# The last three layers of a twelve-layer model in one loop over the steps of a sort

## Chip, cores and metric

The kernel runs on one core of a Trainium2 chip. The metric is the device time of one execution in microseconds (us). An engine is named as the profile names it: PE is TensorE, DVE is VectorE, ACT is ScalarE, POOL is GpSimd, SP issues transfers.

## The reference

Twelve residual layers run over x, 32 tiles of 128 tokens by 128 features. Each layer is `x = x + f(layernorm(x))`. The change touches only the last three:

```python
def sparsemax(z):                       # attention over 32 patterns, 16 heads
    z_sorted = -jnp.sort(-z, axis=-1)
    cum = jnp.cumsum(z_sorted, axis=-1)
    support = 1.0 + k * z_sorted > cum
    k_sup = jnp.sum(support, axis=-1, keepdims=True)
    tau = (jnp.take_along_axis(cum, k_sup - 1, axis=-1) - 1.0) / k_sup
    return jnp.maximum(z - tau, 0.0)
# layer 9:  A = sparsemax(scale * (h @ Wq + bq) . keys); out = (A @ values) @ Wo + bo
# layer 10: probs = softmax(h . ctx / 32) * dropout_mask; out = (probs @ ctx) @ Wout.T + bout
# layer 11: x_scale = max(amax(|h|), 1e-6) / 127; x_q = clip(round(h / x_scale), -128, 127)
#           out = (x_q @ weight_q.T) * x_scale * weight_scale + bias
```

## The kernel before

x stays in the on-chip memory for all twelve layers. A layer walks over eight groups of four tiles, so a `128x512` operand is one group. Each layer is a function of its own, written as one instruction list per engine; semaphores order the engines, and every engine takes its own list strictly in the order of the code. A layer ends with a barrier of all engines. Layers 9, 10 and 11 are `sparse_attention`, `attention1(cross=True)` and `quantized`.

**Layer 9.** `sparse_attention` finds the threshold tau by sorting 64 rows of 32 scores per token. The sort is 15 merge steps on DVE (`STEPS`, lines 3375 and 3376: one `max` and one `min` instruction each, over half of the elements). In ten of the steps (`KEEPS`) ACT copies the ends that the step does not compare (line 3295, `keep_ends`), and the step behind it waits for that copy. Then come a running sum (L3385), a multiplication by 1/k (L3386) and a maximum (L3389), which gives tau; DVE subtracts tau from the scores (L3402) and ACT clips them at zero (L3255). PE turns the clipped scores (L3216), multiplies by the values (L3221) and by the output weights in 64 small matmuls (L3227), and turns the result back (L3233). ACT empties each of these from PSUM (L3260, L3265, L3271). While DVE sorts group i, the other engines finish group i-1 and prepare the scores of group i+1 (L3201, L3204, L3207; copies L3278, L3282, L3287). Where ACT does which copy between its `keep_ends` is written out by hand.

**Layers 10 and 11.** Each handles its eight groups in a loop that is one group deep: layernorm on DVE with the power -1/2 on POOL (L130), then a chain that goes back and forth between the engines. In layer 10 it is turn h (L2327), scores (L2351), maximum and subtraction on DVE (L2480, L2481), `exp` on ACT (L2429), sum and dropout mask on DVE (L2486, L2489), turn (L2361), values (L2372), division on DVE (L2496), turn (L2381), output (L2386), two additions on DVE. In layer 11: layernorm, magnitude on ACT (L3497), maximum and scale (L3528 to L3531), round (L3536 to L3539), turn and product (L3472, L3480), two scalings on DVE (L3546, L3551), and two additions on POOL (L3579, L3583). The last store follows the last addition.

Of the kernel before, what the change touches and what calls it, by code (L numbers as in the profile page):

```python
# [14 lines left out]
ALU = mybir.AluOpType  # L15
# [3084 lines left out]
def sparse_attention(nc, name, x, const, w, at):  # L3100

    S = 32
    ROWS = GROUP * HEADS
    LI = 16  # L3110
    scale = float(HD) ** -0.5
    with ExitStack() as ctx:
        L = Layer(nc, ctx, name, at.side)
        stats = L.sbuf("stats", [T, GROUP, 6])
        moments = L.sbuf("moments", [T, GROUP, 2])
        pad = L.sbuf("pad", [T, 1])
        rstd = L.sbuf("rstd", [T, GROUP])
        h = L.sbuf("h", [T, GROUP, D])
        h_t = L.sbuf("h_t", [D, GROUP * T])
# [7 lines left out]

# [3 lines left out]
        tau = L.sbuf("tau", [T, ROWS])  # L3131
# [3 lines left out]
        p_misc = L.psum("p_misc", [T, BANK])  # L3135
        p_q = L.psum("p_q", [T, BANK])
        p_out = L.psum("p_out", [T, GROUP, D])
        p_s = [L.psum(f"p_s{n}", [T, BANK]) for n in range(4)]
        stats_ready = L.sem("stats_ready")
        rstd_ready = L.sem("rstd_ready")  # L3140
        normed = L.sem("normed")
        trans = L.sem("trans")
        h_t_ready = L.sem("h_t_ready")
# [4 lines left out]
        shifted = L.sem("shifted")  # L3148
        clipped = L.sem("clipped")
# [7 lines left out]
        dve_order = L.sem("dve_order")  # L3157
# [5 lines left out]
        started = lambda i: not (isinstance(i, int) and i == 0)  # L3163
# [3 lines left out]
        def step_buffers(q, n):  # L3167

            return (srt[(n - 1) % 2][:, :, :] if n else z[:, q, :, :]), srt[n % 2][:, :, :]
# [12 lines left out]

        with nc.Block() as block:
            @block.sync
            def _(sp):
                at.fetch(sp)

            @block.tensor
            def _(pe):
                pe.wait_ge(at.loaded, at.count)  # L3190
                nc.tensor.matmul(p_misc[:, 0:S], w["wk"][:, :], w["key_t"][:, :], start=True, stop=True)\
                    .then_inc(kv_done, 1)
                pe.wait_ge(kv_ready, 2)
                nc.tensor.matmul(p_misc[:, 0:D], k_rep[:, :, :], w["wv"][:, :], start=True, stop=True).then_inc(kv_done, 1)
                pe.wait_ge(kv_ready, 3)

                def before(j):

                    pe.wait_ge(normed, j + 1)
                    for u in range(GROUP):  # L3200
                        last = nc.tensor.transpose(p_misc[:, u * T:(u + 1) * T], h[:, u, :], const["ident"][:, :])  # L3201
# [34 lines left out]
                def body(i, p, last_group):  # L3236
                    if started(i):
                        pe.wait_ge(z_ready, GROUP * (i + 1))
                        behind(i - 1, 1 - p)
# [696 lines left out]
```

## Time and profile before

| | us |
|---|---|
| median of 3 runs | 3240.82 (3239.86 to 3245.16) |
| the profiled execution, its own time | 3239.51 |
| its span | 3237.7 |
| layers 9, 10 and 11 in the span | 2643.2 to the end, 594.5 |

The span is the stretch from the first to the last instruction of the profiled execution, and all positions below count from its start. The clock of a stretch is a share of PE's full 2.4 GHz. Two views matter. One gives the busy time of each engine in a stretch (the four stretches below are layer 9's start, its sorts and end, layer 10, and layer 11); an engine that is busy nearly all of it bounds that stretch, while three that are each half busy point to a chain that passes from one to the next. The other lists instructions in order of time, so that a start minus the start before it gives what an instruction really takes of its engine, overlap and gap included.

### The profile page before, as it was taken

How to read it: one execution, taken by the hardware profiler on the slowest of the kernel's cores; microseconds unless marked ns; L12 is line 12 of the kernel's file. 1: busy time of each engine (PE TensorE's matmuls, PEld its weight loads, DVE VectorE, ACT ScalarE, POOL GpSimd, SP SyncE). 2: the span in 40 equal slices, each digit the busy share in tenths (PEclk: the TensorE clock that was granted, in tenths of full speed). 3: DMA queues.
4: the chain of work that ended last, by engine and by line, in shares of the span. 5: the costliest groups of instructions: out<-in, count | busy, mean ns of one | idle time of the engine just before them, and what ended most of it. 6: DMA issues, size and time to landing. Idle time of an engine off the chain costs nothing. (4 is left out here: it accounts for less than half of the span.)

```text
span 3237.7 us, 53191 instructions
## 1 busy us (share of the span) xinstructions
PE 2502.4 (77%) x20516; PEld 1453.8 (45%) x20516; DVE 2098.6 (65%) x4141; ACT 1392.3 (43%) x2771; POOL 604.3 (19%) x581
## 2 busy tenths in 40 slices
PE   6777779999699799979979996799779943443461
PEld 3544546666344344435534444456545521332351
DVE  7989945555687455557654434688732249999657
ACT  5565547777222122223334432498613313433311
POOL 2342511111000133324410000111140120000003
PEclk8888879999799899979979998799879976767665
DMA  1000010000000000010000000200101100000110
GB/s 59 2 2 1 2 39 4 8 8 1 4 1 1 31 2 2 2 45 12 9 4 1 0 1 18 89 9 11 47 32 33 39 17 0 1 1 0 37 44 26
DMA packets 41988, 51.90 MB, mean 16 GB/s; under 512 B 9291, under 2 KB 30868, under 8 KB 40724
## 3 DMA queue, kind: packets, MB, share of 16 engines
q1 hardware_dynamic: 39700, 44.39, 4.3%
q0 software_dynamic: 2048, 4.20, 0.4%
q8 instruction: 164, 2.69, 0.4%
q14 instruction: 76, 0.62, 0.1%
HBM read 39.39 MB, written 9.18 MB: 15 GB/s over the span
## 5 line engine op out<-in xcount | busy, mean ns | idle before, releaser
L130 POOL TENSOR_TENSOR l_rstd<-l_moments,const_minus_half 128x4 f32<-128x4 f32 x104 | 115.6, 1111 | 1535.1 <-DVE l_moments L124 1530.0
L1426 PE MATMUL l_p_gate<-l_h_t,w_wg 128*128 128x512 f32 x400 | 209.0, 605 | 0.0
L1449 PE MATMUL l_p_out<-l_hidden,w_wd 128*128 128x512 f32 x400 | 204.4, 594 | 2.5 <-DVE l_hidden L1719 2.4
L804 DVE TENSOR_REDUCE l_top<-l_ring 128x8 f32<-128x1024 f32 x128 | 150.9, 1221 | 79.6 <-PE l_ring L638 79.5
L2956 DVE SCALAR_TENSOR_TENSOR l_mix<-l_decay,l_cb 128x1024 f32<-128x1024 f32 x128 | 173.4, 1370 | 27.1 <-ACT l_decay L2840 22.9
L2840 ACT ACTIVATE l_decay<-l_p_ring 128x1024 f32<-128x1024 f32 x128 | 129.8, 1026 | 129.3 <-PE l_p_ring L2734 128.3
L350 ACT ACTIVATE l_probs<-l_probs,l_minus_top 128x128 f32<-128x128 f32 x512 | 156.8, 393 | 33.6 <-DVE l_minus_top L410 33.6
L1719 DVE TENSOR_TENSOR l_hidden<-l_act_out,l_p_spread 128x512 f32<-128x512 f32 x128 | 85.8, 686 | 128.9 <-ACT l_act_out L1547 128.7
L3216 PE MATMUL l_p_s<-const_ident,l_z 128*128 128x128 f32 x128 | 27.9, 409 | 177.5 <-ACT l_z L3255 177.5
L1209 DVE TENSOR_REDUCE l_minus_top<-l_p_score 128x4 f32<-128x1024 f32 x64 | 78.3, 1224 | 105.8 <-PE l_p_score L1037 102.2
L136 DVE TENSOR_SCALAR l_h<-x_res,l_moments,l_rstd 128x128 f32<-128x128 f32 (+1 forms) x384 | 112.6, 357 | 45.5 <-POOL l_rstd L130 45.2
L1547 ACT ACTIVATE l_act_out<-l_p_gate,w_eb 128x512 f32<-128x512 f32 x128 | 85.6, 686 | 98.3 <-PE l_p_gate L1426 98.2
L753 ACT ACTIVATE l_probs_t<-l_ring 128x1024 f32<-128x1024 f32 x64 | 62.0, 1022 | 149.2 <-PE l_ring L662 149.2
L3375 DVE TENSOR_TENSOR l_srt<-l_srt 128x1024 f32<-128x1024 f32 (+3 forms) x112 | 115.8, 1034 | 14.8 <-ACT l_srt L3295 11.0
L753 ACT ACTIVATE l_probs_t<-l_ring,l_mask_col 128x1024 f32<-128x1024 f32 x64 | 67.8, 1111 | 121.9 <-PE l_ring L662 121.9
L1140 ACT ACTIVATE l_probs<-l_p_score,l_minus_top 128x256 f32<-128x256 f32 x256 | 118.3, 484 | 1.7 <-DVE l_minus_top L1209 1.7
L888 POOL TENSOR_TENSOR l_spread_q<-l_q_t,const_slot_of 128x512 f32<-128x512 f32 x64 | 66.7, 1042 | 278.0 <-PE l_ring L662 278.0
L3376 DVE TENSOR_TENSOR l_srt<-l_srt 128x1024 f32<-128x1024 f32 (+3 forms) x112 | 114.9, 1026 | 0.0
L1449 PEld LDWEIGHTS l_p_out<-l_hidden,w_wd 128*128 128x128 f32 x400 | 75.3, 190 | 84.4 <-issue 52.3
L3216 PEld LDWEIGHTS l_p_s<-const_ident,l_z 128*128 128x128 f32 x128 | 25.7, 223 | 183.3 <-issue 154.8
L1426 PEld LDWEIGHTS l_p_gate<-l_h_t,w_wg 128*128 128x128 f32 x400 | 72.2, 193 | 78.1 <-issue 64.3
L405 DVE TENSOR_TENSOR l_probs<-l_p_score,l_bias 128x1024 f32<-128x1024 f32 x64 | 78.0, 1219 | 37.3 <-PE l_p_score L258 37.3
(471 smaller groups left out, 6260.9 us busy)
## 6 DMA issues: line engine op xcount, KB each, us to landing
l_c_t<-in_ctx_t SPq DMA_DIRECT2D x24, 256.0 KB, 2.8
l_rows_in<-l_zero SPq DMA_DIRECT2D x1, 2432.0 KB
l_tile_h<-l_rows_in SPq DMA_DIRECT2D x38, 64.0 KB, 1.9
l_rows_out<-l_tile_y SPq DMA_DIRECT2D x38, 64.0 KB, 1.5
w_mask<-in_mask SPq DMA_DIRECT2D x1, 2048.0 KB, 9.2
w_wg<-in_l2f_wg SPq DMA_DIRECT2D x1, 2048.0 KB
w_wu<-in_l2f_wu SPq DMA_DIRECT2D x1, 2048.0 KB
w_wd<-in_l2f_wd SPq DMA_DIRECT2D x1, 2048.0 KB
```

Of the source, the lines that this page charges most:

```text
L130: return nc.gpsimd.tensor_tensor(rstd[:, :], moments[:, :, 1], minus_half[:, 0:moments.shape[1]], ALU.pow)
L136: last = nc.vector.tensor_scalar(h[:, u, :], x[:, i * count + u, :], moments[:, u, 0:1], rstd[:, u:u + 1], ALU.subtract, ALU.mult)
L350: last = nc.scalar.activation(probs[:, g % 4, k, :], probs[:, g % 4, k, :], ACT.Exp, bias=minus_top[:, g % 4, k:k + 1])
L753: nc.scalar.activation(probs_t[:, b % 2, half * HALF:(half + 1) * HALF, :], turned_buffer(b, half)[:, :, :, :].rearrange("p a r q -> p (a ...
L804: nc.vector.tensor_reduce(top[:, b % 2, half * HALF:(half + 1) * HALF, 0], s, AX.X, ALU.max)\
L1140: last = nc.scalar.activation(probs[:, g % 2, k, :], p_score[g % 2][:, odd, b * KEYS:(b + 1) * KEYS], ACT.Exp, bias=minus_top[:, g % 2, k: ...
L1426: nc.tensor.matmul(p_gate[k % 2][:, :], w["wg"][:, s, :], h_t[:, g % 4, :], start=True, stop=True)\
L1449: nc.tensor.matmul(p_out[:, :], w["wd"][:, s, :], hidden[:, k % 4, :], start=(s == 0), stop=(gated and s == steps - 1)).then_inc(down, 1)
L2840: nc.scalar.activation(decay[:, g % RING, :, :], p_ring[slot % 2][:, :, :], ACT.Exp).then_inc(evicted, 1)
L2956: nc.vector.scalar_tensor_tensor(mix[:, g % RING, :, :], decay[:, g % RING, :, :], 1.0, bcast(cb[:, i % 2, n // 4, :], [T, QH, T], 1), ALU ...
L3375: nc.vector.tensor_tensor(da, a, b, ALU.max)
L3376: last = nc.vector.tensor_tensor(db, a, b, ALU.min)
```

## The change

The three functions become one, `sparse_cross_quantized`. Every engine's list is now written by a loop over a step number `g`; a sort has 18 steps (15 merge steps, running sum, multiplication, maximum), and `group_at(g, s)` says which group is at place `s` of a timetable that starts with its sort. Layer 10 of a group begins 27 steps behind the start of its sort, and layer 11 at 39. So, while group k+1 is sorted, group k finishes layer 9 and starts layer 10, and group k-1 goes through layer 11.

Four pieces of work also move. The threshold is no longer subtracted by DVE and clipped by ACT before the turning: its negative is turned to rows (`turn_tau`), and PE adds it while turning the scores, by a second matmul with `spread`, which repeats each row of 64 thresholds 32 times; ACT clips while it empties PSUM. The layernorm of layers 9 and 10 is applied by ACT with a per-row scale and bias, for which DVE makes a small `offset`. The sum of the softmax comes out of ACT's `exp` (`accum_out`), and ACT also does the division and the scaling of layer 11 by row. POOL's two additions of layer 11 go to DVE.

```diff
-def sparse_attention(nc, name, x, const, w, at):
+def sparse_cross_quantized(nc, name, x, const, w, at, aps):
...
+        SORTED = len(STEPS)
+        SCAN, INVERSE, TAU = SORTED, SORTED + 1, SORTED + 2
+        PERIOD = TAU + 1
+        BEFORE, BEHIND, IN_CROSS, IN_QUANT = -15, TAU + 1, TAU + 10, TAU + 22
+        def group_at(g, step):
+            k, off = divmod(g - step, PERIOD)
+            return k if off == 0 and 0 <= k < NG else None
...
+                def turn_tau(k):
+                    pe.wait_ge(tau_ready, k + 1)
+                    nc.tensor.transpose(p_out[0:ROWS, 0, :], minus_tau[:, k % 2, :], const["ident"][:, :]).then_inc(tau_turned, 1)
+                def transposes(k):
+                    pe.wait_ge(tau_t_ready, k + 1)
+                    pe.wait_ge(z_ready, GROUP * min(k + 2, NG))
                     for b in range(4):
                         for u in range(GROUP):
-                            last = nc.tensor.transpose(p_s[b][:, u * T:(u + 1) * T], z[:, q, row:row + 4, :],
-                                                       const["ident"][:, :])
+                            nc.tensor.matmul(out, z[:, k % 2, row:row + 4, :], const["ident"][:, :], start=True, stop=False)
+                            last = nc.tensor.matmul(out, spread[:, row:row + 4, :], tau_t[:, :], start=False, stop=True)
                         last.then_inc(turned, 1)
...
+                for g in range(FIRST, END):          # PE; step k of the timetable runs before step k+1
+                    BEHIND: turn_tau;  BEHIND + 1: transposes;  BEHIND + 2, + 3: weigh
...
```

The loop of each engine is a list of such places, shortened here to the places (in brackets: the step of the sort in which the place falls). `BEHIND` is 18 (step 0), `BEFORE` -15 (step 3), `IN_CROSS` 27 (step 9), `IN_QUANT` 39 (step 3).

```
PE:   turn_tau (0) transposes (1) weigh (2, 3) project (5) turn_out (7) turn_h (6) queries (7) scores (8)
      cross_turn_h (12) cross_scores (13) cross_transposes (16) cross_values (17) turn_att (0) cross_output (1)
      turn_quant (8) product (9)
ACT:  keep_ends (each of KEEPS, first in its step) copy_tau (1) clip_turned (2, 3) copy_weighed (4, 5)
      copy_projected (6, 7) norm_apply SPARSE (6) copy_h (7) copy_queries (8) copy_scores (9, 10)
      norm_apply CROSS (12) cross_copy_h (13) exponent (15) cross_copy_turned (17) divide (0) copy_att (1)
      magnitude (6) copy_quant (9) scale_output (10)
DVE:  sort (its step) scan (15) inverse (16) threshold (17) add_output (8) norm_stats SPARSE (3)
      norm_offset SPARSE (5) norm_stats CROSS (9) norm_offset CROSS (11) cross_top (14) cross_mask (16)
      cross_add (2) norm_stats QUANT (3) quant_apply (5) largest (7) round_h (8) quant_add (11)
```

```diff
-                def clip(j, q):
-                    nc.scalar.activation(z[:, q, :, :], z[:, q, :, :], ACT.Relu).then_inc(clipped, 1)
+                def norm_apply(layer, k):
+                    for u in range(GROUP):
+                        last = nc.scalar.activation(h[layer][:, u, :], x[:, k * GROUP + u, :], ACT.Identity,
+                                                    bias=offset[layer][:, u:u + 1], scale=rstd[layer][:, u:u + 1])
+                def clip_turned(k, b):
+                    act.wait_ge(turned, 4 * k + b + 1)
+                    nc.scalar.activation(a_t[:, b, :], p_s[b][:, :], ACT.Relu).then_inc(turned_out, 1)
+                def exponent(k):
+                    for u in range(GROUP):
+                        last = nc.scalar.activation(probs[:, u, :], p_cross[:, u * T:(u + 1) * T], ACT.Exp, bias=minus_top[:, u:u + 1],
+                                                    scale=cross_scale, accum_out=total[:, u:u + 1])
+                def divide(k):
+                        last = nc.scalar.activation(att[:, u, :], p_cross[:, u * D:(u + 1) * D], ACT.Copy, scale=total[:, u:u + 1])
+                def scale_output(k):
+                        last = nc.scalar.activation(out8[:, u, :], p_quant[:, u * D:(u + 1) * D], ACT.Copy, scale=scale8[:, u:u + 1])
...
-                    nc.vector.tensor_tensor(z[:, p, :, :], z[:, p, :, :], bcast(tau[:, :], [T, ROWS, S], 2), ALU.subtract)\
-                        .then_inc(shifted, 1)
+                def cross_add(k):
+                    dve.wait_ge(cross_out, k + 1)
+                    nc.vector.tensor_tensor(update[:, :, :], by_token(p_cross[:, :]), bcast(w["cross_bo"][:, :], [T, GROUP, D], 1),
+                                            ALU.add).then_inc(cross_added, 1)
+                    dve.wait_ge(cross_added, k + 1)
+                    order.then(nc.vector.tensor_tensor(rows_of(k), rows_of(k), update[:, :, :], ALU.add))
+                def largest(k):
+                    dve.wait_ge(mag_ready, k + 1)
+                def quant_add(k):
+                    dve.wait_ge(quant_scaled, k + 1)
...
-LAYERS = {0: layer0, 9: layer9, 1: layer1, 6: layer6, 10: layer10, 11: layer11, ...}
+LAYERS = {0: layer0, 9: layer9, 1: layer1, 6: layer6, ...}
-ORDER = tuple(range(12))
+ORDER = tuple(range(10))
```

How the instructions stand now. First PE between the thresholds of one group and its output matmuls, before; `l_p_s` are the four PSUM banks of the group, `l_z` its scores, `l_o_of` the weighed values:

```order
L3207 MATMUL l_p_s<-l_keys,l_q_t 128x512 x4
L3216 MATMUL l_p_s<-const_ident,l_z 128x128 x16
L3221 MATMUL l_p_s<-l_a_t,l_vals_of 128x512 x4
L3227 MATMUL l_p_s<-l_o_of,w_wo 128x128 x64
L3233 MATMUL l_p_out<-const_ident,l_y_t 128x128 x4
```

And PE at the same place now (the pair of L3304 and L3305 stands 16 times; `l_p_cross` is the one PSUM bank of layer 10):

```order
L3347 MATMUL l_p_cross<-const_ident,l_probs 128x128 x4
L3354 MATMUL l_p_cross<-l_ctx_v,l_probs_t 128x128 x4
L3296 MATMUL l_p_out<-const_ident,l_minus_tau 64x128
L3361 MATMUL l_p_cross<-const_ident,l_att 128x128 x4
L3304 MATMUL l_p_s<-const_ident,l_z 128x128
L3305 MATMUL l_p_s<-l_tau_t,l_spread 128x128
...
L3367 MATMUL l_p_cross<-w_cross_wo,l_att_t 128x128 x4
L3310 MATMUL l_p_s<-l_a_t,l_vals_of 128x512 x4
L3317 MATMUL l_p_s<-l_o_of,w_wo 128x128 x64
```

The output matmuls of layer 10 of the group before (L3367) now stand behind all 16 pairs. On DVE the piece that waits for them is this one, from the maximum that gives tau to the fourth step of the next sort (`l_update` is layer 10's output with its bias):

```order
L3631 TENSOR_REDUCE l_minus_tau<-l_srt 128x64
L3611 TENSOR_TENSOR l_srt<-l_z 128x1024
L3612 TENSOR_TENSOR l_srt<-l_z 128x1024
L3611 TENSOR_TENSOR l_srt<-l_srt 128x512x2
L3612 TENSOR_TENSOR l_srt<-l_srt 128x512x2
L3611 TENSOR_TENSOR l_srt<-l_srt 128x512
L3612 TENSOR_TENSOR l_srt<-l_srt 128x512
L3652 TENSOR_TENSOR l_update<-l_p_cross,w_cross_bo 128x512
L3655 TENSOR_TENSOR x_res<-x_res,l_update 128x512
L3611 TENSOR_TENSOR l_srt<-l_srt 128x256x4
```

Three merge steps stand between the threshold and the addition of layer 10; before, the sort was followed by the subtraction L3402 and nothing of another layer. On ACT the same stretch of a sort, from the copy of the third merge step (L3476 is `keep_ends` now) to that of the eighth:

```order
L3476 COPY l_srt<-l_srt 128x512x2
L3442 ACTIVATE l_a_t<-l_p_s 128x512 x4
L3476 COPY l_srt<-l_srt 128x256x2x2
L3446 COPY l_o_of<-l_p_s 128x32x16 x2
L3476 COPY l_srt<-l_srt 128x256x2
L3446 COPY l_o_of<-l_p_s 128x32x16 x2
L3451 ACTIVATE l_y_t<-l_p_s,w_bo 128x4x4x8 x2
L3432 ACTIVATE l_h<-x_res,l_offset,l_rstd 128x128 x4
L3510 ACTIVATE l_mag<-l_h 128x512
L3476 COPY l_srt<-l_srt 128x128x2x4
```

The copies of the weighed values (L3446) have moved from ahead of the second `keep_ends` to behind the second and third, and the magnitude of layer 11 (L3510), for which DVE waits in step 7, stands behind the first copies of the projection (L3451).

## Rows read from the trace of the kernel before

**Rows 1.** Stretches: us, busy PE, PEld, DVE, ACT, POOL, PE clock, DMA, GB/s.
```profile
2643.00:2662.00 19.00, 10.21 (x19) 4.49 (x19) 9.42 (x41) 3.62 (x6) 2.06 (x2) 0.56 0.03 7
2662.00:3049.98 387.98, 148.18 (x1346) 101.37 (x1346) 349.17 (x364) 158.71 (x226) 6.04 (x6) 0.70 0.00 1
3050.00:3155.40 105.40, 61.89 (x288) 53.92 (x288) 58.02 (x178) 19.78 (x33) 8.06 (x8) 0.64 0.20 62
3155.40:3237.70 82.30, 13.76 (x64) 8.49 (x64) 60.23 (x185) 9.73 (x16) 28.35 (x24) 0.50 0.07 26
```

**Rows 2.** Timeline of one sort period: start us, us, engine, line, operation.
```profile
2708.44 1.22 DVE L3375 TENSOR_TENSOR l_srt<-l_z 128x1024 f32<-128x1024 f32 x1
...
2715.35 1.22 DVE L3375 TENSOR_TENSOR l_srt<-l_srt 128x1024 f32<-128x1024 f32 x1
...
2725.55 0.96 DVE L3375 TENSOR_TENSOR l_srt<-l_srt 128x768 f32<-128x768 f32 x1 [0.55 <-ACT l_srt L3295]
...
2739.55 4.42 DVE L3385 TENSOR_TENSOR_SCAN l_srt<-l_starts,l_srt 128x2048 f32<-128x2048 f32 x1
...
2746.33 2.29 DVE L3389 TENSOR_REDUCE l_tau<-l_srt 128x64 f32<-128x2048 f32 x1
...
2749.26 2.28 DVE L3402 TENSOR_TENSOR l_z<-l_z,l_tau 128x2048 f32<-128x2048 f32 x1
...
2752.78 0.17 DVE L124 TENSOR_SCALAR l_moments<-l_moments 128x4 f32<-128x4 f32 x1
...
2754.07 1.12 DVE L136 TENSOR_SCALAR l_h<-x_res,l_moments,l_rstd 128x128 f32<-128x128 f32 x4 [1.12 <-POOL l_rstd L130]
2755.10 1.22 DVE L3375 TENSOR_TENSOR l_srt<-l_z 128x1024 f32<-128x1024 f32 x1
```

**Rows 3.** Timeline of PE: the small matmuls at either clock.
```profile
2706.97 3.65 PE L3216 MATMUL l_p_s<-const_ident,l_z 128*128 128x128 f32 x16 [19.12 <-ACT l_z L3255]
...
3075.40 1.06 PE L2351 MATMUL l_p_score<-l_k_t,l_h_t 128*128 128x128 f32 x8
...
3138.53 1.91 PE L2351 MATMUL l_p_score<-l_k_t,l_h_t 128*128 128x128 f32 x8
```

**Rows 4.** Timeline of PE: the large matmuls of layer 9 at either clock.
```profile
2681.50 6.35 PE L3207 MATMUL l_p_s<-l_keys,l_q_t 128*128 128x512 f32 x8 [0.78 <-ACT l_q_t L3282]
...
2710.41 3.77 PE L3221 MATMUL l_p_s<-l_a_t,l_vals_of 128*128 128x512 f32 x8
...
2718.16 5.19 PE L3227 MATMUL l_p_s<-l_o_of,w_wo 32*128 32x128 f32 x128 [3.96 <-ACT l_o_of L3265]
...
2728.24 3.70 PE L3207 MATMUL l_p_s<-l_keys,l_q_t 128*128 128x512 f32 x8 [0.78 <-ACT l_q_t L3282]
```

**Rows 5.** Timeline of ACT in one sort period.
```profile
2713.24 1.13 ACT L3295 COPY l_srt<-l_srt 128x1024 f32<-128x1024 f32 x1 [1.99 <-DVE l_srt L3376]
...
2714.25 3.85 ACT L3265 COPY l_o_of<-l_p_s 128x512 f32<-128x512 f32 x4
...
2723.37 1.14 ACT L3271 ACTIVATE l_y_t<-l_p_s,w_bo 128x128 f32<-128x128 f32 x4 [3.08 <-PE l_p_s L3227]
```

**Rows 6.** Groups of instructions by form: count, busy, mean ns of one.
```profile
L2815 ACT ACTIVATE l_conv<-l_p_ring,w_conv_b,w_conv_w 128x512 f32<-128x512 f32 x32 | 25.1, 784 | 0.0
L3282 ACT ACTIVATE l_q_t<-l_p_q,l_scaled_bq 128x512 f32<-128x512 f32 x8 | 5.5, 687 | 7.6 <-PE l_p_q L3204 7.6
```

**Rows 7.** Groups of the last three layers: DVE beside POOL's additions.
```profile
L3536 DVE TENSOR_TENSOR l_q<-l_h,l_amax 128x512 f32<-128x512 f32 x8 | 11.4, 1421 | 0.3
L3551 DVE TENSOR_TENSOR l_out<-l_out,w_scale 128x512 f32<-128x512 f32 x8 | 5.5, 686 | 0.0
```

**Rows 8.** Timeline in layer 0 and at the very end: POOL.
```profile
112.66 1.22 DVE L2956 SCALAR_TENSOR_TENSOR l_mix<-l_decay,l_cb 128x1024 f32<-128x1024 f32 x1
112.82 2.22 POOL L130 TENSOR_TENSOR l_rstd<-l_moments,const_minus_half 128x4 f32<-128x4 f32 x1 [8.71 <-DVE l_moments L124]
...
3233.48 1.26 POOL L3583 TENSOR_TENSOR x_res<-x_res,l_out 128x512 f32<-128x512 f32 x1
```

More of the change, by code:

```diff
@@ L3130, in sparse_attention @@
         starts = L.sbuf("starts", [T, ROWS, S])
-        tau = L.sbuf("tau", [T, ROWS])
+        minus_tau = L.sbuf("minus_tau", [T, 2, ROWS])
+        tau_t = L.sbuf("tau_t", [ROWS, T])
+        spread = L.sbuf("spread", [ROWS, ROWS, S])
+        offset = [L.sbuf(f"offset{n}", [T, GROUP]) for n in range(2)]
         a_t = L.sbuf("a_t", [T, 4, GROUP * T])
@@ L3234, in behind @@
                     last.then_inc(out_done, 1)
[L3236 to L3239, printed above, removed]
-                    if not last_group:
-                        if not started(i):
-                            pe.wait_ge(z_ready, GROUP)
-                        before(i + 1)
-                before(0)
-                for i in range(NG):
-                    body(i, i % 2, i == NG - 1)
@@ new lines, in turn_att, with cross_output @@
+                def turn_att(k):
+                    pe.wait_ge(cross_divided, k + 1)
+                    for u in range(GROUP):
+                        last = nc.tensor.transpose(p_cross[:, u * T:(u + 1) * T], att[:, u, :], const["ident"][:, :])
+                    last.then_inc(att_turned, 1)
+                def cross_output(k):
+                    pe.wait_ge(att_t_ready, k + 1)
+                    for u in range(GROUP):
+                        last = nc.tensor.matmul(p_cross[:, u * D:(u + 1) * D], att_t[:, u * T:(u + 1) * T],
+                                                w["cross_wo"][:, :], start=True, stop=True)
+                    last.then_inc(cross_out, 1)
@@ new lines, in turn_quant, with product @@
+                def turn_quant(k):
+                    pe.wait_ge(rounded, k + 1)
+                    if k >= 1:
+                        pe.wait_ge(quant_scaled, k)
+                    for u in range(GROUP):
+                        last = nc.tensor.transpose(p_quant[:, u * T:(u + 1) * T], q[:, u, :], const["ident"][:, :])
+                    last.then_inc(q_turned, 1)
+                def product(k):
+                    if k == 0:
+                        pe.wait_ge(wq_ready, 1)
+                    pe.wait_ge(q8_t_ready, k + 1)
+                    for u in range(GROUP):
+                        last = nc.tensor.matmul(p_quant[:, u * D:(u + 1) * D], q8_t[:, u * T:(u + 1) * T], wq8[:, :],
+                                                start=True, stop=True)
+                    last.then_inc(quant_out, 1)
@@ L3404, in _, with norm_stats, norm_offset @@
[L3404 to L3407 removed]
+                def norm_stats(layer, k):
+                    layernorm_stats(nc, dve, order, x, k, stats[layer], moments[layer], pad[layer]).then_inc(stats_ready[layer], 1)
+                def norm_offset(layer, k):
+                    dve.wait_ge(rstd_ready[layer], k + 1)
+                    nc.vector.scalar_tensor_tensor(offset[layer][:, :], moments[layer][:, :, 0], -1.0, rstd[layer][:, :],
+                                                   ALU.mult, ALU.mult).then_inc(offset_ready[layer], 1)
```

731 lines of the change are left out of this document (403 added, 328 removed).

## Prediction

> **What bounds the kernel now.** I read the busy times by stretch first, since the shares of the whole page average over twelve layers. In the sorts of layer 9, DVE is busy 349.2 of 388.0 us; PE and ACT are busy 148 and 159 us [rows 1]. That stretch is bound by DVE. In layers 10 and 11 no engine is: DVE is busy 58.0 of 105.4 and 60.2 of 82.3 us, PE 61.9 and 13.8 us [rows 1]. There the chain between the engines sets the pace. So the three layers hold 477 us of DVE work in 594.5 us, and the question is whether the idle 117 us can be closed.
>
> The timeline of one sort period tells what DVE does in it. A period is 46.66 us (2708.44 to 2755.10). The 15 merge steps take 31.1 us, of which 0.55 and some 0.1 are waits for ACT's copies; sum, multiplication and maximum take 9.1 us (2739.55 to 2748.62). Then come an addition of 0.6, the subtraction of the threshold 2.2, the layernorm's statistics 1.5 (2751.46 to 2752.95), 1.1 of waiting for POOL and 1.0 of applying it [rows 2]. The sort alone is thus 30.5 + 9.1 = 39.6 us.
>
> **DVE's work after the change.** Gone from a period are the subtraction, the wait for POOL and the application; an addition (0.7 with its semaphore), the statistics (1.5) and a small offset (0.2) stay: 42.0 us. Layer 10 costs DVE 58.0 / 8 = 7.25 us a group, less a subtraction, a sum and a division of 0.69 each [rows 7] and an application of 1.1 [rows 2]: 4.1. Layer 11 costs 60.2 / 8 = 7.5, less one scaling of 0.69 and the 0.73 by which the rounding multiplication was slowed beside POOL's additions (1.42 against 0.69 [rows 7]), plus the two additions from POOL at 0.69: 7.5. With 0.5 for gaps behind semaphores a full period would hold 54.1 us of DVE. With nothing else in the way the stage would be a start of 21, periods of 42, 45, 5 x 54.1 and 52.4, and an end of 67, in all 498 us. That is 96 us less than now.
>
> **Why I do not expect that.** The engines take their lists in order, and the lists meet at three places. I walk through one full period; t = 0 is the end of the reduction that gives the thresholds.
>
> *PE and the turning.* Before, 16 transposes took 3.65 us at the low clock [rows 3], 0.23 each. Now there are 16 pairs of fp32 matmuls, and an fp32 matmul of this size is two instructions: 8 instructions took 1.91 us at 1.2 GHz and 1.06 us at 2.4 GHz [rows 3], 0.24 and 0.13 each. 64 of them are 15.3 or 8.5 us. PE comes to them from short work with gaps, so at the low clock; in the trace the clock rose 3.4 us after the transposes began (2706.97; the matmuls at 2710.41 run at the high clock [rows 3, 4]), and in the scores at 2681.50 only after nearly 6 us [rows 4]. I take 4.6 us at the low clock and the rest at the high one: 10.5 us. The trace has no fp32 matmul with 64 rows of weights; I price it as one with 128, and nothing in the rows allows less than one instruction's 0.13.
>
> *Stall 1, at `cross_add`.* The mask of layer 10 is ready 2.4 us before t = 0. From there: turn 1.1, copy 0.7, values 2.0, division 1.2 (four instructions in 1.14 [rows 5]), turning of the attention 1.1, so PE reaches the pairs at t = 4.0 and leaves them at 14.5; the output matmuls of layer 10, behind them, end at 15.6. DVE has run three merge steps (2708.44 to 2715.35 [rows 2]) and stands at `cross_add` from t = 6.9. It waits 8.7 us and leaves the two additions at A = 17.2. Behind it wait the sort and every copy of ACT that needs a step.
>
> *Stall 2, at `largest`.* Steps 3 to 7 take 9.6 us (2715.35 to 2725.55 less 0.6 of waits [rows 2]), two sets of statistics 3.0, offset and application 1.2: DVE asks for the magnitude at A + 13.8. ACT's list up to it: `keep_ends` behind step 3, then two copies of weighed values until A + 5.4 (3.85 us for four [rows 5]), `keep_ends` behind step 4 and two more until A + 9.3. PE's 64 matmuls take 5.2 [rows 4] until 14.6; then ACT's copies 0.7, the layernorm 1.6 and the magnitude 0.7: A + 17.6. DVE waits 3.8 us.
>
> *Stall 3, at `quant_add`.* The maximum and its three small instructions take 1.3, step 8 1.9, an addition 0.7, rounding 1.5 (until A + 23.1); then step 9 2.1, statistics 1.5, steps 10 and 11 3.7 and an offset 0.2: DVE reaches `quant_add` at A + 30.7. PE makes queries (2.1) and then the scores from A + 23.5. These took 6.35 us at a mostly low and 3.70 at the high clock [rows 4]; I take 5.6. Turning, copy, product, two score copies and the scaling bring it to A + 32.7: 2.0 us of wait. At the high clock this stall is gone.
>
> What follows until the next threshold is clean: 2.1 for `quant_add`, and 17.0 for steps 12 to 17 with maximum and mask. So the period ends at A + 51.8 = 69.0 us, 15 us above DVE's work.
>
> *What hides.* The four `exp` with a sum (1.1 us by the nearest row [rows 5], twice that if a sum costs another instruction each) run beside the running sum of 4.4 us; without that cover they would cost their length eight times, 9 to 18 us. The layernorm of layer 10 on ACT runs beside step 12, and the three powers have two merge steps each. The transfers of layer 10 move to the start and to one group per period, and a store of a group goes out while the next is sorted; layer 10 used 0.20 of the DMA engines for 105 us [rows 1], so they fit into a period three times. SP's list waits for `added` before it loads the group three further on; that group's data is needed a whole period later. The two barriers between the layers, some 2 us, are in the 594.5 already.
>
> *ACT's new work.* A scale and a bias per row cost ACT about 0.1 us each: 784 ns with both, 687 with one [rows 6]. Four instructions with one take 1.14 us [rows 5], with both I take 1.6. Applying the norm took DVE 1.12 [rows 2]. The Trainium skill, page "ScalarE: Activation LUTs", section "Rules for kernel authors", advises VectorE over ScalarE for additions and multiplications, and the same page puts a pointer operand at 93 ns, with which the trace agrees. By its figures the four would be an estimated 1.6 us too, and the rule speaks against the move only where ACT is late, as it is at stall 2.
>
> **The sum.** The start takes 19 us before [rows 1]; the filling of `spread` (2048 elements; the cheapest and the dearest instruction of that size would be about 1 and 2.3) and the slower application make it 21.3. The first sort waits 2 us for scores at the low clock: 44. The second has no rest of layer 10, but its step 8 waits for the `keep_ends` that stands behind the projection, some 6.6 us: 55. Five full periods: 345. The last one, without a next group: 64. The end: up to `cross_add` of the group before 17; its layer 11 beside the last projection until 35; then the last group's layer 10, 18 from its first copy (turn and copy 2, scores 2, maximum 1, `exp` 1.6, mask 0.7, turn and copy 2, values 2, division 1.2, turn, copy and output 4, additions 1.5), and its layer 11, 13: 66 us, and 3 from the last addition to the end of the span, as now [rows 8]: 69. In all 598.5, against 594.5: 4.0 us more. The profiled execution took 3239.5, 1.3 less than the median of the runs; so 3243.5 beside it, and 3245 as a median.
>
> **The rivals.**
> 1. *The clock is mostly high* (faster). PE has more to do per us than before, when the sorts ran at a mean of 0.70 of full speed [rows 1]. Then the pairs take 8.5, the steps ahead of them 1.4 less, and stall 3 goes: 63.6 us a period, and 3210 in all; halfway between is 3228. Against it: layer 10, with PE busy 62 of 105 us, had 0.64 [rows 1]. I take 3222 for this case. It decides for faster from about 2 us saved in each of six periods.
> 2. *The clock stays low through the pairs.* 15.3 instead of 10.5, seven times and once in the end: 3245 + 34, about 3279.
> 3. *DVE and POOL block each other.* All merge steps read two tensors on chip and now run beside POOL's power. The rows speak both ways: POOL's power took 2.22 us when DVE's two-tensor instruction had started first, and that one its usual 1.22 [rows 8]; but the rounding was slowed by 0.73 beside a POOL addition [rows 7]. If each of some 22 powers costs DVE 0.73, it is 16 us: 3261. The Trainium skill, page "SBUF — State Buffer", section "Who interferes with whom", has the one that issues second wait for the whole of the other; by that rule either could be the loser, and the trace agrees with both sides of it.
> 4. *It does what it says*: no stall, DVE at 54.1 a period, 498 us, 3144. This needs PE through the pairs and layer 10's output by t = 6.9, that is 3 us for 64 instructions.
>
> **How the numbers follow.** Chances: forecast 0.40, rival 1 0.30, rival 2 0.12, rival 3 0.08, rival 4 0.05, and 0.05 for further waits of 15 to 30 us. The forecast's own range is 3234 to 3256. About 0.2% (6.5 us) is what a measurement of this kernel can tell from no change. Faster: nearly all of rival 1, rival 4 and a little of the forecast, 0.35. Within 0.2%: 0.27. Slower: 0.38. The range from 3213 to 3277 leaves out rival 4, the far ends of 1 and 2.
>
> **What the profile would show.** Right: sort periods of 65 to 73 us; DVE waiting 7 to 10 us for the matmuls of `cross_out` once per period from the third sort on, with the 64 instructions of the pairs just before them; 3 to 5 us for ACT's magnitude; up to 3 for ACT's `out8`; no merge step longer beside POOL's power. Wrong: periods near 54 us, or a wait at the copies of the ends that is longer than these three. What would upset the forecast most is the clock in the pairs, since each 0.05 us per instruction is 3.2 us a period.

## The result, and the profile after

The changed kernel took 3353.57 us (median of 4 runs, 3352.19 to 3355.07), the kernel before 3242.29 us (4 runs, 3239.86 to 3245.16). The ratio is 1.034, with a 95% interval from 1.0327 to 1.0353: 111 us slower, far above the forecast of 3245 and outside its range.

The common stage first, by stretch of the profile of the changed kernel (columns as in [rows 1]; the first stretch still holds 10.8 us of the layer before, and the third row is the stage alone), with the line of DVE at which the stage begins, in the timeline of the kernel before and in that of the changed one:

```profile
2643.00:2665.00 22.00, 8.59 (x28) 4.20 (x26) 12.34 (x39) 3.85 (x8) 1.05 (x1) 0.72 0.22 72
2665.00:3352.00 687.00, 428.63 (x2100) 284.52 (x2100) 418.00 (x677) 225.28 (x461) 32.48 (x23) 0.60 0.03 10
2653.76:3352.78 699.02, 431.11 (x2108) 286.20 (x2108) 425.14 (x702) 227.35 (x465) 33.53 (x24) 0.60 0.04 13
```

```profile
2643.23 0.87 DVE L118 BATCH_NORM_STATS2 l_stats<-x_res 128x6 f32<-128x128 f32 x4 [1.47 <-PEq L41]
```

```profile
2653.76 0.87 DVE L118 BATCH_NORM_STATS2 l_stats<-x_res 128x6 f32<-128x128 f32 x4 [1.47 <-PEq L41]
```

DVE is busy 425 us in the stage where it was busy 477 [rows 1], as the change intends. But PE has gone from 234 us (10.2, 148.2, 61.9 and 13.8 in [rows 1]) to 431, at a granted clock of 0.60. From its first line to the end of the span the stage now takes 3352.8 - 2653.8 = 699.0 us; it was 3237.7 - 2643.2 = 594.5. The other 10.5 us of this profile lie ahead of the stage, in layers that the change doesn't touch.

One full period of DVE, from one maximum that gives the thresholds to the next:

```profile
2946.60 2.25 DVE L3631 TENSOR_REDUCE l_minus_tau<-l_srt 128x64 f32<-128x2048 f32 x1
...
2954.68 1.06 DVE L3612 TENSOR_TENSOR l_srt<-l_srt 128x512 f32<-128x512 f32 x1
2977.82 0.69 DVE L3652 TENSOR_TENSOR l_update<-l_p_cross,w_cross_bo 128x512 f32<-128x512 f32 x1 [22.08 <-PE l_p_cross L3367]
...
2997.82 0.69 DVE L3659 TENSOR_REDUCE l_amax<-l_mag 128x4 f32<-128x512 f32 x1 [5.12 <-ACT l_mag L3510]
...
3011.92 0.69 DVE L3673 TENSOR_TENSOR l_out<-l_out,w_quant_scale 128x512 f32<-128x512 f32 x1 [1.22 <-ACT l_out L3521]
...
3028.51 2.25 DVE L3631 TENSOR_REDUCE l_minus_tau<-l_srt 128x64 f32<-128x2048 f32 x1
```

The period is 81.9 us, where I had 69.0. Of it 28.4 are the three stalls that the prediction named, and 53.5 is DVE's work. The second and third stall have about the size forecast (5.1 for 3.8, 1.2 for 2.0); the first is 22.1 where I had 8.7. What stands ahead of L3367 on PE, in PE's own timeline, with the loads of weights below:

```profile
2952.65 0.64 PE L3304 MATMUL l_p_s<-const_ident,l_z 128*128 128x128 f32 x2
2953.22 0.79 PE L3305 MATMUL l_p_s<-l_tau_t,l_spread 64*128 64x128 f32 x2
2953.94 0.79 PE L3304 MATMUL l_p_s<-const_ident,l_z 128*128 128x128 f32 x2
2954.66 0.79 PE L3305 MATMUL l_p_s<-l_tau_t,l_spread 64*128 64x128 f32 x2
```

```profile
2953.21 0.50 PEld L3305 LDWEIGHTS l_p_s<-l_tau_t,l_spread 64*128 64x128 f32 x2 [0.23 <-issue]
2953.94 0.50 PEld L3304 LDWEIGHTS l_p_s<-const_ident,l_z 128*128 128x128 f32 x2 [0.22 <-issue]
```

```profile
2952.65:2975.64 22.99, 22.99 (x66) 15.81 (x65) 3.06 (x3) 3.50 (x5) 0.00 (x0) 0.50 0.01 2
```

Read the starts, not the durations: a matmul (two instructions) starts every 0.72 us, and ahead of each the loads of weights pause 0.22 us for "issue", that is for nothing that the profile shows. The last row gives the pairs as a whole: 22.99 us, at a granted clock of 0.50 (1.2 GHz) from end to end. I had 10.5 us and a clock that rises after 4.6. The other seven sets of pairs in this profile take 22.98 to 23.15 us, also at 0.50.

The waits of DVE in the stage say the same in sum (waited for: us in total, times, longest):

```profile
DVE l_update L3652 <- PE l_p_cross L3367: 170.3, 8, 29.0
DVE l_amax L3659 <- ACT l_mag L3510: 33.8, 8, 5.1
DVE l_srt L3611 <- ACT l_srt L3476: 24.7, 5, 13.7
DVE l_srt L3611 <- ACT l_z L3467: 13.1, 1, 13.1
DVE l_out L3673 <- ACT l_out L3521: 10.2, 7, 3.7
```

### The profile page after: what moved, and what is told of

Its sections match the earlier page's. It is cut to its first block and busy times, and to the rows that moved or that the text cites. A ratio compares the mean times of both kernels' runs of the same rounds, so it can differ in the third digit from the quotient of the medians.

```text
span 3352.8 us, 53700 instructions
## 1 busy us (share of the span) xinstructions
PE 2703.9 (81%) x20883; PEld 1575.5 (47%) x20908; DVE 2048.2 (61%) x4076; ACT 1427.8 (43%) x2955; POOL 593.4 (18%) x565
## 5 line engine op out<-in xcount | busy, mean ns | idle before, releaser
L130 POOL TENSOR_TENSOR l_rstd<-l_moments,const_minus_half 128x4 f32<-128x4 f32 x104 | 125.5, 1207 | 1663.9 <-DVE l_moments L124 1658.9
L136 DVE TENSOR_SCALAR l_h<-x_res,l_moments,l_rstd 128x128 f32<-128x128 f32 (+1 forms) x320 | 94.8, 360 | 29.8 <-POOL l_rstd L130 29.5
L3305 PE MATMUL l_p_s<-l_tau_t,l_spread 64*128 64x128 f32 x256 | 101.5, 498 | 0.0
```

Of the source, the lines that this page charges most:

```text
L130: return nc.gpsimd.tensor_tensor(rstd[:, :], moments[:, :, 1], minus_half[:, 0:moments.shape[1]], ALU.pow)
L3305: last = nc.tensor.matmul(out, spread[:, row:row + 4, :], tau_t[:, :], start=False, stop=True)
```

## The experiments

Each is the changed kernel with the edit shown. They were run in three sets of four, each set with the kernel before beside it on the same chip; its medians were 3243.29, 3239.23 and 3243.41 us, and each ratio below is to the one of its own set. The third set (the runs of two, both kernels with the early magnitude, and the last one) ran on another chip than the first two. Where kernels of different sets are compared, the length of the stage in the profile is given too, because the layers ahead of it, which are the same code, differ by up to 11.7 us between the profiles.

**The rows of the weights.** Theory A: in the pairs, weights of 128 rows (`z`) and of 64 (`spread`) take turns, and the turn is what costs.

```
-spread = L.sbuf("spread", [ROWS, ROWS, S])
-tau_t = L.sbuf("tau_t", [ROWS, T])
+spread = L.sbuf("spread", [T, ROWS, S])
+tau_t = L.sbuf("tau_t", [T, T])
...
+nc.vector.memset(tau_t[ROWS:T, :], 0.0)
```

> The second operand pair of the threshold is widened from 64 to 128 rows (rows 64 to 127 are zero), nothing else changes. Theory A, the change between matmuls with 128 and with 64 rows of weights holds the weight load back until the matmul before it is through, and PE is then too thinly loaded to be given the high clock: the 64 instructions fall from 23.0 us (0.36 each) to the pace of the other fp32 matmuls, 0.24 at the low and 0.13 at the high clock, some 8.5 to 11 us with the clock rising on the way; that is 12 us less in each of seven periods and in the end, about 3257 us. Theory B, the second matmul of a pair waits because it adds to the place in PSUM that the first has just written: the pace stays at 0.36, 23 us, and the time at 3353.

Measured: 3226.1 us, ratio 0.9948 (0.993 to 0.9966). PE's timeline in its pairs, first and in the middle, and the stretch of all of them:

```profile
2904.85 0.63 PE L3304 MATMUL l_p_s<-const_ident,l_z 128*128 128x128 f32 x2
2905.28 0.63 PE L3305 MATMUL l_p_s<-l_tau_t,l_spread 128*128 128x128 f32 x2
...
2908.42 0.39 PE L3305 MATMUL l_p_s<-l_tau_t,l_spread 128*128 128x128 f32 x2
2908.64 0.39 PE L3304 MATMUL l_p_s<-const_ident,l_z 128*128 128x128 f32 x2
```

```profile
2904.85:2913.56 8.71, 8.71 (x66) 8.71 (x65) 3.09 (x3) 3.50 (x5) 0.00 (x0) 0.81 0.01 3
```

A matmul starts every 0.43 us, then every 0.22 from 3.3 us into the pairs on, when the granted clock has gone to its upper level (2.4 GHz). With as many instructions and as many columns, and half the rows of the spread only zeros, 23.0 us have become 8.7, and the kernel is 127 us faster than the changed one. Theory B falls, since the two matmuls of a pair still add to one place. Theory A holds, and pays more than I had expected (3257 us): a period is shorter by 17 us and not 12, since the pairs alone are 14.3 us shorter and what stands behind them is waited for less. But two things changed at once: the pace at a given clock, and the clock. The next runs part them.

**Fewer turns.** The same matmuls in another order, four with `z`, then four with the spread:

```
-for b in range(4):
-    for u in range(GROUP):
-        matmul(out, z...); matmul(out, spread...)
+for u in range(GROUP):
+    for b in range(4): matmul(out, z...)
+    for b in range(4): matmul(out, spread...)
```

> The same 16 pairs, but in runs of four: the four score matmuls of a tile for the four banks, then its four threshold matmuls. The 64-row operand stays. Theory A (change of rows): only 8 changes instead of 32, so within a run 0.24 or 0.13 per instruction and a loss at each change: 12 to 17 us for the 64 instructions. Theory B (adding to a place just written): no matmul adds to what its predecessor wrote, so 8.5 to 11 us. ACT gets all four banks at the end. By both the period falls by 6 to 12 us: 3260 to 3310 us. If neither holds: 23 us and slower than 3353, since the banks come late.

Measured: 3289.67 us, ratio 1.0145 (1.0123 to 1.0167). Its pairs:

```profile
2929.21:2945.08 15.87, 15.87 (x65) 14.08 (x65) 3.10 (x3) 2.90 (x5) 0.00 (x0) 0.50 0.01 3
```

And with runs of two in place of four:

```
+for u in range(GROUP):
+    for first in (0, 2):
+        for b in (first, first + 1): matmul(out, z...)
+        for b in (first, first + 1): matmul(out, spread...)
```

> Edit: the changed kernel with two matmuls with z as weights, then two with the spread (64 rows), and so on: 16 changes between weights of 128 and of 64 rows a group, where the changed kernel has 32 and interleaved 8. Law to be tested: an fp32 matmul of 128 columns takes 0.427 us at 1.2 GHz and each change of the rows of the weights 0.28 to 0.29 more, which gives 23.0 us for the changed kernel and 15.9 for interleaved, as measured. Here it gives 32 x 0.427 + 16 x 0.285 = 18.2 us and some 3310 us for the kernel. Rival (there is no price per change, it is a matter of matmuls into the same bank one after the other): as fast as interleaved, 15.9 us and 3290.

Measured: 3308.79 us (one run), and for the pairs:

```profile
2931.10:2949.34 18.24, 18.24 (x65) 14.64 (x64) 3.10 (x3) 3.13 (x5) 0.00 (x0) 0.50 0.01 2
```

In the sets shown all three orders stay at 0.50, so only the number of turns differs (changes of rows from one matmul to the next, the last one before the output matmuls among them): 32 turns 22.99 us, 16 turns 18.24, 8 turns 15.87. That is 32 x 0.43 = 13.7 us and 0.27 to 0.29 for each turn. The value for 16 was forecast from the other two and met to 0.04 us. The rival, that it is the two matmuls into one bank one after the other that cost, wanted 15.9 there.

One set of pairs out of the eight of the interleaved kernel, the last, ran otherwise:

```profile
3224.27:3226.40 2.13, 2.13 (x10) 1.91 (x10) 0.00 (x0) 0.59 (x1) 0.00 (x0) 0.50 0.00 0
3226.50:3233.87 7.37, 7.37 (x56) 6.52 (x55) 0.00 (x0) 0.56 (x2) 0.00 (x0) 1.00 0.01 2
```

```profile
3228.44 1.16 PE L3307 MATMUL l_p_s<-l_tau_t,l_spread 64*128 64x128 f32 x8
3229.53 1.16 PE L3304 MATMUL l_p_s<-const_ident,l_z 128*128 128x128 f32 x8
3230.61 1.16 PE L3307 MATMUL l_p_s<-l_tau_t,l_spread 64*128 64x128 f32 x8
```

Here the clock rose 2.2 us after the pairs began and stayed up to their end, in 9.6 us altogether. A run of four matmuls starts every 1.09 us; four at the pace of k128's upper clock would be 0.89, so a turn costs 0.2 us at 2.4 GHz.

**Rows or order, for the clock.** Interleaved with the padded operands:

> Edit: the order of the interleaved kernel (four matmuls with z as weights, then four with the spread as weights) and the spread and the turned threshold padded with zeros to 128 rows, as in k128. It separates order from rows: interleaved had 15.87 us for the 64 instructions at a granted clock of 0.50 throughout, k128 8.71 us with the clock rising after 3 us. Theory R (what keeps the clock at 0.50 is that half the weights fill only 64 rows): the clock rises as in k128, the pairs take 8.7 us, the kernel 3226 us. Theory O (it is the order): 15.9 us at 0.50 and 3290 us. With 64 against 8 changes of operands and 128 rows throughout, no pace should differ from k128 by more than 0.01 us per instruction.

Measured: 3231.25 us (one run). The pairs:

```profile
2907.65:2916.33 8.68, 8.68 (x66) 8.68 (x65) 3.11 (x3) 2.20 (x3) 0.00 (x0) 0.82 0.01 4
```

The order of interleaved with 128 rows gives the clock and time of k128 (the stage is 574.0 us long in the one profile and 573.9 in the other). So what the clock goes with here is the rows of the weights and not the order. The other way round, both matmuls with 64 rows:

```
-matmul(out, z[:, k % 2, row:row + 4, :], ident[:, :], start=True, stop=False)
+matmul(out, z[0:ROWS, k % 2, row:row + 4, :], ident[0:ROWS, :], start=True, stop=False)
```

> Edit: the order of the changed kernel (pairs), but the matmul with z contracts over 64 rows as well, like the one with the spread; it leaves out the scores of half of the tokens. Theory A (the change between weights of 128 and 64 rows is what adds 0.11 us an instruction): there is none, so the pace is 0.25 us an instruction at 1.2 GHz, 15.9 us in all if the clock stays at 0.50, 8.7 if it rises; the kernel 3290 or 3226 us. Theory A2 (a weight load of 64 rows is slow by itself): 23 us or more and 3353. Theory R (weights of 64 rows keep the clock down) wants the 0.50 here above all.

Measured: 3276.79 us (one run), and for the pairs, with PE's timeline at their start:

```profile
2922.74:2936.68 13.94, 13.94 (x65) 13.72 (x64) 2.96 (x3) 3.51 (x5) 0.00 (x0) 0.50 0.01 1
```

```profile
2922.74 0.79 PE L3304 MATMUL l_p_s<-const_ident,l_z 64*128 64x128 f32 x2
2923.32 0.63 PE L3305 MATMUL l_p_s<-l_tau_t,l_spread 64*128 64x128 f32 x2
2923.75 0.63 PE L3304 MATMUL l_p_s<-const_ident,l_z 64*128 64x128 f32 x2
```

Weights of 64 rows are not slow by themselves: the pace is 0.43 us a matmul again, and the pause appears only where 64 rows follow 128 rows and back. The 13.94 us are below the 15.9 that I had expected, because I had not yet taken the 8 turns out of interleaved's figure. And the clock stays at 0.50 in all eight sets, as it does in 31 of the 32 sets of the other four kernels with 64-row weights (the one exception is shown above); in the 32 sets of the four kernels with padded operands it rose 1.0 to 4.8 us after the pairs began. So a thinly loaded PE, as the expectation of k128 had it, is not the reason: here the matmuls follow each other without a pause, and the clock stays low all the same. Theory A's second form (a slow load) falls. Few rows alone are not enough to keep the clock down, though: the projection's weights have 32 rows, in four strips of rows in turn, and in the kernel before the clock rose during it, in the stretch that begins 3.8 us after its start at 2718.16 [rows 4]:

```profile
2722.00:2724.00 2.00, 1.34 (x49) 1.15 (x44) 1.97 (x3) 0.63 (x3) 0.00 (x0) 1.00 0.00 0
```

What the chip counts for the clock is thus not settled by these runs.

**What the threshold matmul costs in all.** Without L3305, so that the thresholds are not subtracted at all:

```
 matmul(out, z..., start=True, stop=True)
-matmul(out, spread..., start=False, stop=True)
```

> Leaves out the subtraction of the threshold (the 16 matmuls with spread); the score matmuls stay as they are. By A and B the 32 instructions run at 0.24 falling to 0.13: 5.5 to 7.7 us, a period about 16 us shorter, some 3220 to 3235 us. Theory C, an fp32 matmul against the identity takes 0.36 per instruction whatever stands beside it: 11.5 us, about 3262 us.

Measured: 3200.51 us (one run). The thresholds' matmuls thus cost the changed kernel 153 us; padded they still cost 26. Theory C falls: the 32 instructions take 5.1 us in a full period, not 11.5. The kernel is 20 us below the range that I gave, since a period is 20.5 us shorter (61.45) and not 16: besides the 17.9 us of the pairs, the output matmuls behind them run at a higher clock, and the second and third stall shrink as well.

**The list of PE around the stall.** With the output matmuls of layer 10 ahead of the pairs:

```
+if (k := group_at(g, IN_CROSS + 10)) is not None:
+    cross_output(k)
 if (k := group_at(g, BEHIND + 1)) is not None:
     transposes(k)
```

> PE makes the output of layer 10 (L3367) before the 16 pairs and not behind them; nothing else changes. The wait of DVE at cross_add (22 us a period) falls to under 1 us. Theory D, the stall only moves: ACT may not do the copy of merge step 4 until it has clipped all four banks, which come out of PE no earlier than 30 us behind the threshold, so DVE waits some 15 to 16 us at merge step 5; a period is about 4 us shorter, near 3330 us. Theory E, the order on PE was the cause: the 22 us go, near 3200 us.

Measured: 3323.86 us, ratio 1.0233 (1.0201 to 1.0265). Its waits of DVE:

```profile
DVE l_srt L3611 <- ACT l_srt L3476: 127.5, 15, 17.8
DVE l_amax L3659 <- ACT l_mag L3510: 57.5, 8, 29.4
DVE l_update L3652 <- PE l_p_cross L3367: 15.8, 2, 9.0
```

Of 170 us of waiting for L3367, 154 are gone, and 30 us of time: 103 turn up at the copies of the ends, which stand behind four clips on ACT that wait for the pairs, and 24 at the magnitude. So theory D holds. It was not the place of the output in the list that cost most but the length of the pairs. With short pairs a larger part of the stall can be won:

> Edit: k128 and output_first together. In k128 a period is 64.9 us and DVE waits 6.75 us at cross_add, for the output matmuls that stand behind the 64 instructions. Put ahead of them, they end before DVE arrives, so this stall goes, but the copy of the ends that merge step 5 needs stands behind four clips on ACT, which wait for the pairs. By my walk DVE then waits some 2.4 us there instead: 4.3 us saved a period, about 3193 us. Rival (the stall only moves): 3220 to 3226. Rival (the wait at the magnitude absorbs it): no less than 3215.

Measured: 3204.29 us, ratio 0.9898 (0.9879 to 0.9917), 22 us less than k128 (23.0 in the stage). The wait at the copies is 1.6 us in a full period (expected 2.4), but the wait for the magnitude grew from 4.12 to 5.97 and took part of the gain, so my 3193 was 11 too low:

```profile
2901.57 1.13 DVE L3612 TENSOR_TENSOR l_srt<-l_srt 128x768 f32<-128x768 f32 x1 [1.61 <-ACT l_srt L3476]
2914.51 0.69 DVE L3660 TENSOR_REDUCE l_amax<-l_mag 128x4 f32<-128x512 f32 x1 [5.97 <-ACT l_mag L3510]
```

**The common function without the new way of subtracting.** The threshold is subtracted by DVE again:

```
 def threshold(k):
     nc.vector.tensor_reduce(minus_tau[:, k % 2, :], ranked, AX.X, ALU.max, negate=True)...
+    nc.vector.tensor_tensor(z[:, k % 2, :, :], z[:, k % 2, :, :], bcast(minus_tau...), ALU.add)
 def transposes(k):
-    matmul(out, z...); matmul(out, spread...)
+    nc.tensor.transpose(out, z[:, k % 2, row:row + 4, :], ident)
```

> Edit: the common function and its order stay, but the threshold goes back to DVE as before the change: one addition of minus the threshold over 128x2048 (2.3 us) behind the maximum, and 16 transposes instead of 64 instructions; the turning and copying of the threshold go. Theory A (the threshold on TensorE is what costs the change its gain): DVE has 2.3 us more a period, the transposes run from t = 4.0 to 7.7 and the output of layer 10 ends at 8.8, before DVE stands at cross_add at 9.2. The period is that of the kernel without threshold matmuls (59.8) less its stall of 3.2 and plus 2.3: 58.9, and 3193 us. Rival B (the common order of three layers is bad by itself): over 3243. Rival C (padding is as good as this): 3226.

Measured: 3196.26 us, ratio 0.9864 (0.9847 to 0.9881), against 3193 expected. A period is 61.2 us, though, and not 58.9: the 59.8 from which I had worked is 61.45 in the trace. So the time was met closer than the working deserved. In PE's timeline the pairs' place is taken by

```profile
2898.36 3.62 PE L3297 MATMUL l_p_s<-const_ident,l_z 128*128 128x128 f32 x16
2901.77 1.10 PE L3359 MATMUL l_p_cross<-w_cross_wo,l_att_t 128*128 128x128 f32 x8
```

and the stall at `cross_add` is gone from the full periods. The common function is a gain; the way of subtracting turned it into a loss.

**The next stall.** DVE still waited some 5 us a period for the magnitude, which stands on ACT behind copies that wait for the projection. Moved ahead of them, with the application of layer 9's norm:

```
+if (k := group_at(g, IN_QUANT + 3)) is not None:
+    magnitude(k)
+if (k := group_at(g, BEFORE + 3)) is not None:
+    norm_apply(SPARSE, k)
 for b in range(4):
     ... clip_turned, copy_weighed, copy_projected
```

> Edit: subtract_on_dve, and in ACT's list the magnitude and the application of layer 9's norm go ahead of the copies of the projection, for which ACT waits some 5 us with both of them behind. DVE's second stall (4.75 us in a full period, at the largest magnitude) should go. DVE then comes to quant_add earlier by that, while PE's chain of scores moves up only by the 2.2 us that it waited for the norm, so some 2.5 us come back as stall 3. Expected: 2.2 us less a period or more, 3178 us. Rival (PE's chain behind the projection bounds the period, stall 3 takes it all): 3196.

Measured: 3169.89 us, ratio 0.9772 (0.9756 to 0.9788), 8 us below the 3178 expected. Most of these 8 us are not the edit's: the 3178 was worked from 3196 in another set, and in this profile the stage begins 8.3 us earlier than in that one. The stage itself went from 543.9 to 522.6 us, 21.3 less where I had expected 18, and a period from 61.2 to 58.1. In a full period one wait is left, again at a copy of the ends behind the copies of the projection, and none at `quant_add`:

```profile
2903.84 0.96 DVE L3594 TENSOR_TENSOR l_srt<-l_srt 128x768 f32<-128x768 f32 x1 [2.44 <-ACT l_srt L3462]
2931.90 2.25 DVE L3614 TENSOR_REDUCE l_minus_tau<-l_srt 128x64 f32<-128x2048 f32 x1
...
2990.00 2.25 DVE L3614 TENSOR_REDUCE l_minus_tau<-l_srt 128x64 f32<-128x2048 f32 x1
```

The same edit on the padded version:

> Edit: k128_output_first, and in ACT's list the magnitude and the application of layer 9's norm ahead of the copies of the projection. The stall at the largest magnitude is 5.97 us there. Expected: about 3 us less a period, 3183 us, against 3178 for the version with the subtraction on DVE. Rival: the wait comes back whole at quant_add, 3204.

Measured: 3176.84 us, ratio 0.9796 (0.978 to 0.9813), against 3183 expected; 7 us behind the version with the subtraction on DVE, which ran beside it. The stage is 19.6 us shorter than in k128 with the output first, 531.3 for 550.9. Last, the turning of layer 11's rounded rows ahead of the scores on PE:

```
+if (k := group_at(g, IN_QUANT + 5)) is not None:
+    turn_quant(k)
 if (k := group_at(g, BEFORE + 5)) is not None:
     scores(k)
```

> Edit: subtract_on_dve_early_magnitude, and on PE the turning of layer 11's rounded rows goes ahead of layer 9's scores. With the magnitude early, the rounding is done when PE comes to the scores, so the turning should fit without a wait and ACT's copy and the product follow the scores without it: 1.3 us less in the chain to quant_add, 3170 us if that stall ends last. Rival (the turning waits for the rounding and holds up the scores and ACT's copies of z): 3180 or more.

Measured: 3171.72 us, ratio 0.979 (0.9767 to 0.9814), no different from the kernel without it (stage 522.0 and 522.6 us). There was no wait left at `quant_add` in a full period for it to shorten, so my 3170 came out for the wrong reason.

## Why the prediction was wrong

**The step that failed** is the pairs' price: "the trace has no fp32 matmul with 64 rows of weights; I price it as one with 128". With 128 rows this was right, and the pairs of k128 take 8.7 us, inside my bounds of 8.5 and 15.3. With 64 against 128 rows they take 23.0, outside the upper bound. The second step that rests on it, "I take 4.6 us at the low clock and the rest at the high one", failed with it: the clock did not rise at all during the pairs. The parts, per group: 10.5 forecast; 1.8 less, since with 128 rows the clock rises after 3.3 and not 4.6 us, and an instruction then takes 0.11 and not 0.13; 5.0 more, since it stays at 0.50 (13.7 for 8.7); 9.3 more for 32 turns of 0.29. That is 12.5 us a group and 100 us for eight. That the turns and the clock cost this is shown by the runs; why PE pauses at a turn, and why the clock stays down with 64-row weights, stays open.

**It accounts for the miss.** From the first line of the stage to its end I had 598.5 us, and 699.0 were measured: 100.5 more. I forecast the end of the first threshold 65.3 us after the start of the stage; it came after 64.9 (2716.41 + 2.29 - 2653.76). Each stretch that holds one set of pairs is 11.5 to 13 us longer than forecast: the second sort 66.6 for 55, the full periods 81.9 for 69.0, the last sort 76.7 for 64, the end 81.5 for 69.

**What is left.** The profiled execution took 3354.57 us, 111.1 more than the 3243.5 forecast for it. Of these, 100.5 are the stage, and the other 10.5 are those by which the stage begins later in this profile. The same line stands between 2644.2 and 2655.9 us in the profiles of the other kernels here, whose layers 0 to 8 are the same code: between 2646.3 and 2655.9 on the one chip, where interleaved with the padded operands, whose pairs are short, has 2655.4, and between 2644.2 and 2646.7 on the other. So this is no effect of the pairs. What sets it was not tried, and stays open.

**The chain was right.** PE came to the pairs 3.8 us after the threshold (4.0 forecast, though the terms listed for it make 3.7), DVE stood at `cross_add` 6.9 after it, and the three stalls are where they were said to be, in that order, with DVE's own work at 53.5 us (54.1). The magnitude's wait was larger mainly because the projection took 6.2 us, against 5.2 in the forecast. It began at the low clock, but not because the pairs had left it low: the clock had risen 4.5 us behind them, and fell while PE waited 6.4 us for ACT's copies:

```profile
2980.10:2986.90 6.80, 2.32 (x6) 0.77 (x4) 6.58 (x26) 4.01 (x5) 2.39 (x2) 1.00 0.00 0
2987.10:2988.80 1.70, 0.00 (x0) 0.00 (x0) 1.67 (x6) 1.66 (x2) 0.00 (x0) 0.50 0.00 0
2988.81:2995.01 6.20, 6.20 (x128) 6.01 (x128) 3.86 (x6) 0.00 (x0) 0.00 (x0) 0.60 0.01 3
```

In a full period the exponentials with a sum and layer 10's norm on ACT were hidden; layer 9's norm (1.6 us) stands in the magnitude's chain, as the prediction had it. No merge step was longer beside POOL's power.

**Slips in the working.** The terms of the sum make 598.3 and not 598.5. Rival 2's 4.8 us stand eight times, which is 38 and 3283 us, and not 34 and 3279; with either, its middle and not only its far end lies outside the range up to 3277. In the kernel before, the clock rose 3.8 us after the transposes at 2706.97 began, not 3.4. None of this changes the account above.

**The rivals.** Rival 2, a low clock through the pairs, was right about the clock, and its 15.3 us was the dearest that I allowed; pairs of about that length, in interleaved, went with 3290 us. Rival 1 is close to what happens with padded operands: 64.9 us a period in k128 for its 63.6, and 3226 us for its 3222. Rival 3 did not show. Rival 4 asked for no stall and came out as 3144; the best version has one of 2.4 us in a full period and DVE's subtraction of 2.3, and stands at 3170, with its stage 522.6 us long (498 in the rival).

The Trainium skill, page "TensorE: Matmul & The Clock Gate", section "LDWEIGHTS (loading the stationary operand)", says that the load depends on the columns and not on the contracted rows. The trace agrees for loads of one kind (0.43 us a matmul with 64 and with 128 rows). It bears on no mixture, and there the same matmuls took 0.72 us.

## What to carry to other kernels

When a change adds matmuls whose contracted rows differ from those of the matmuls around them, price the turns as well as the matmuls, or pad the operands with zeros to the same rows; here the padding, which adds no instruction to the loop, was worth 127 us. When the trace has no row for a new instruction, allow for a dearer price as well as a cheaper one, and try it by itself. An engine that waits for an item in another engine's list waits for everything that stands ahead of it there: look for the longest item first, and only then at the order. Here shortening the pairs was worth 127 us, and moving the output matmuls ahead of the long pairs 30. And when several edits come in one change, try the parts apart: the common loop, with the norms, the division and the scaling on ACT, gained 43 us (3239.2 to 3196.3; the stage alone 594.5 to 543.9), and the new way of subtracting lost 157 (155 of them in the stage).

## What was not expected of the hardware

- fp32 matmuls of 128 columns with 128-row and 64-row weights in turn: 0.72 us each at 1.2 GHz, against 0.43 with either alone; 0.27 to 0.29 us for each turn, seen as a pause of 0.22 us ahead of the loads of weights. At 2.4 GHz, in the one set of pairs that ran so (the last of the interleaved kernel), a turn cost 0.2 us.
- With half or all of the weights 64 rows high, PE was busy without a gap for 13.9 to 23.0 us and the granted clock stayed at 0.50, in 39 of 40 sets of pairs; in the one other set it rose after 2.2 us and did not fall during the 7.4 us of pairs that followed. With 128 rows throughout it rose in each of 32 sets, 3.3 us after the pairs began in the period shown of k128. Whether rows of zeros and rows of numbers are alike in this in other settings was not tried; here the spread's added rows are zeros and the clock rose.
